# Five of the first loads issued by ScalarE's queue instead of the sync engine's, in a four-layer graph kernel on one core

## What is computed

```python
h = jnp.maximum(_layernorm(x, axis=-1), 0.0)
x = x + _L0_gnn_ref(h, adj, ...)   # H = (adj != 0); relu(conv(h, W1, b1)); layer norm; conv(., W2, b2); + h
h = jnp.maximum(_layernorm(x, axis=-1), 0.0)
x = x + _L1_gnn_ref(h, adj, ...)   # tanh(dinv * A * dinv @ (h @ W) + b)
h = jnp.maximum(_layernorm(x, axis=-1), 0.0)
x = x + _L2_gnn_ref(h, adj, ...)   # scores s = (h @ w) @ a; exp(leaky(8 tanh((s_i + s_j) / 8))) * adj, normalised; @ h @ w
h = jnp.maximum(_layernorm(x, axis=-1), 0.0)
x = x + _L3_gnn_ref(h, adj, ...)   # three times adj @ (x @ W) + b, relu between
```

## Time and profile before

| | |
|---|---|
| median of 3 runs | 1349.94 us (1349.46 to 1351.4) |
| the profiled execution | 1351.4 us, span from first to last instruction 1349.6 us |
| PE busy | 1326.8 us, 98% |
| DVE busy | 1182.8 us, 88% |
| ACT busy | 1048.1 us, 78% |
| POOL busy | 1056.1 us, 78% |
| mean granted clock of TensorE | 0.997 |
| DMA traffic | 64.48 MB, all but the instructions' own on one queue (q1) |

### The profile page before, as it was taken

The page is one execution under the profiler, slowest core; times in us unless marked ns, Lnnn a source line. Parts: engine busy times, 40 slices in busy tenths (PEclk is TensorE's granted clock), DMA queues, the critical chain, the costliest instruction groups (busy, mean ns, idle before and its releaser), DMA issues.

```text
span 1349.6 us, 32286 instructions
## 1 busy us (share of the span) xinstructions
PE 1326.8 (98%) x10680; PEld 1282.2 (95%) x10680; DVE 1182.8 (88%) x3607; ACT 1048.1 (78%) x2632; POOL 1056.1 (78%) x2004
## 2 busy tenths in 40 slices
PE   8899999999999999999999999999999999999988
PEld 7889999999999999999999999999999999999987
DVE  8878898898998898898898898998998998989875
ACT  6776877887887887887887877877877877878864
POOL 7876778778788788788788788788788888888761
PEclk9989999999999999999999999999999999999999
DMA  7011111111111111111111111111111111111100
GB/s 215 21 32 33 44 57 37 48 56 37 48 56 37 48 56 37 48 56 37 48 56 37 48 56 36 49 53 39 49 50 39 52 48 37 56 48 33 33 9 32
DMA packets 83220, 64.48 MB, mean 48 GB/s; under 512 B 40304, under 2 KB 65520, under 8 KB 83056
## 3 DMA queue, kind: packets, MB, share of 16 engines
q1 hardware_dynamic: 83056, 62.43, 15.8%
HBM read 45.62 MB, written 16.78 MB: 46 GB/s over the span
## 4 chain that ended last, share of the span: by engine, by line
PE 89%; DVE 6%; ACT 2%; issue 1%; POOL 1%; DVEq 0%; POOLq 0%; ACTq 0%
PE BANK L351 29%; PE BANK L319 24%; PE BANK L358 14%; PE WIDE L330 8%; PE WIDE L351 8%; PE WIDE L358 4%; PE BANK L304 2%; PE BANK L369 1%; DVE BN_D L535 0%; DVE BN_B L535 0%; DVE BN_A L535 0%; DVE BN_C L535 0%; DVE ULO_B L576 0%; DVE ULO_A L576 0%; ACT H_B L404 0%
## 5 line engine op out<-in xcount | busy, mean ns | idle before, releaser
L576 DVE TENSOR_TENSOR ULO_D<-BANK,UHI_D 128x512 fp32r<-128x512 f32 x96 | 65.6, 684 | 18.6 <-ACT UHI_D L435 18.5
L576 DVE TENSOR_TENSOR ULO_B<-BANK,UHI_B 128x512 fp32r<-128x512 f32 x96 | 65.6, 683 | 17.5 <-ACT UHI_B L435 17.4
L576 DVE TENSOR_TENSOR ULO_A<-BANK,UHI_A 128x512 fp32r<-128x512 f32 x96 | 65.6, 683 | 17.0 <-ACT UHI_A L435 17.0
L576 DVE TENSOR_TENSOR ULO_C<-BANK,UHI_C 128x512 fp32r<-128x512 f32 x96 | 65.5, 683 | 14.1 <-ACT UHI_C L435 14.1
L435 ACT ACTIVATE UHI_C<-BANK 128x512 fp32r<-128x512 f32 x96 | 57.4, 598 | 21.3 <-PE BANK L319 20.1
L435 ACT ACTIVATE UHI_B<-BANK 128x512 fp32r<-128x512 f32 x96 | 57.3, 597 | 20.5 <-PE BANK L319 19.1
L435 ACT ACTIVATE UHI_A<-BANK 128x512 fp32r<-128x512 f32 x96 | 57.4, 598 | 19.5 <-PE BANK L319 18.1
L435 ACT ACTIVATE UHI_D<-BANK 128x512 fp32r<-128x512 f32 x96 | 57.3, 597 | 18.7 <-PE BANK L319 17.4
L705 POOL TENSOR_TENSOR LN_D<-LN_D,MHALF 128x2 f32<-128x2 f32 x80 | 55.7, 696 | 1.3
L705 POOL TENSOR_TENSOR LN_A<-LN_A,MHALF 128x2 f32<-128x2 f32 x80 | 55.7, 696 | 1.3
L705 POOL TENSOR_TENSOR LN_C<-LN_C,MHALF 128x2 f32<-128x2 f32 x80 | 55.6, 695 | 1.3
(11 more groups left out here) (487 smaller groups left out, 5761.5 us busy)
## 6 DMA issues: line engine op xcount, KB each, us to landing
X_A<-in_xs SPq DMA_DIRECT2D x16, 256.0 KB, 2.5
X_B<-in_xs SPq DMA_DIRECT2D x16, 256.0 KB, 2.7
X_C<-in_xs SPq DMA_DIRECT2D x16, 256.0 KB, 2.6
X_D<-in_xs SPq DMA_DIRECT2D x16, 256.0 KB, 2.6
out_rows<-O_A SPq DMA_DIRECT2D x16, 256.0 KB, 2.0
out_rows<-O_B SPq DMA_DIRECT2D x16, 256.0 KB, 2.0
out_rows<-O_C SPq DMA_DIRECT2D x16, 256.0 KB, 2.1
out_rows<-O_D SPq DMA_DIRECT2D x16, 256.0 KB, 2.0
```

Source lines behind the costliest of these rows:

```text
L576: nc.vector.tensor_tensor(ULO[s][:, 0:J * D], bank(s, step, k)[:, :], UHI[s][:, 0:J * D].bitcast(F32), ALU.subtract).then_inc(sem(f"l{step ...
```

## The change

The five loads leave SP's program. ACT issues them, in the same order among themselves, ahead of the first step of its own list. Nothing else is changed: every load has the same source, destination and semaphore, and who waits for it waits for the same count.

```diff
             load("A")
-            sp.dma_start(W1[:, :, :], w1t).then_inc(sem("w1_loaded"), 16)
-            sp.dma_start(COLS[:, :], cols).then_inc(sem("cols_loaded"), 16)
             load("B")
-            sp.dma_start(W2[:, :, :], w2t).then_inc(sem("w2_loaded"), 16)
-            sp.dma_start(L2WT[:, :, :], l2wt).then_inc(sem("l2wt_loaded"), 16)
-            sp.dma_start(B1[:, :], b1.partition_broadcast(P)).then_inc(sem("b1_loaded"), 16)
             load("C")
             sp.dma_start(B2[:, :], b2.partition_broadcast(P)).then_inc(sem("b2_loaded"), 16)
             load("D")
...
+            nc.scalar.dma_start(W1[:, :, :], w1t).then_inc(sem("w1_loaded"), 16)
+            nc.scalar.dma_start(COLS[:, :], cols).then_inc(sem("cols_loaded"), 16)
+            nc.scalar.dma_start(W2[:, :, :], w2t).then_inc(sem("w2_loaded"), 16)
+            nc.scalar.dma_start(L2WT[:, :, :], l2wt).then_inc(sem("l2wt_loaded"), 16)
+            nc.scalar.dma_start(B1[:, :], b1.partition_broadcast(P)).then_inc(sem("b1_loaded"), 16)
             run("ACT", parts)
```

## The result

The changed kernel takes 1353.09 us in the median of 20 runs (1351.81 to 1356.54), the kernel before 1350.26 us (1349.46 to 1354.94). The ratio is 1.0017, with a 95% interval of 1.0009 to 1.0025: slower by some 2.3 us (1.2 to 3.4). That is just inside the 0.2% that I had set as the bound of no change. The median of 1353.09 itself lies 0.1 us above my range; reckoned with the ratio from the 1349.94 that I forecast from, it is 1352.2, inside it. In the later measurements one run of before (1473.29 us) and one of `e7_cols_only` (2694.45 us) were far slower than all the others, and no ratio counts them.

What follows compares the result with a forecast made beforehand. PE, busy 1326.8 of 1349.6 us, was taken to bound the kernel, with the change touching only the start. Terms 0 + 0 + 0 + 0.4 us, added to the median of 1349.94, gave 1350.3 us; range 1347.5 to 1353.0.

Steps and rivals of the forecast that it cites:

- The class: Whole kernel: faster (below 1347.2 us) 0.11, within 0.75, slower (above 1352.6 us) 0.14.
- part 4: Start: two queues share the DMA engines and TF_A lands later; cost 0.4 us.
- rival (b): Start: W1 goes whole ahead of TF_A, delaying it 1.5 us; +1.0 us, 1350.9 us; chance 0.20.
- Part 1: SP's queue: five issues leave, so stream B's loads go about 1.0 us earlier, later streams' about 2.5; worth 0.
- Part 2: Start: the five loads arrive earlier, COLS by up to 1.7 us, with DVE still waiting for UHI_A; gain 0.
- Part 3: ACT's start: five issues, 2.3 us, fit into its 4.17 us of idle time before BHT_A; cost 0.
- d = 0.95 us: Start: assumed delay of TF_A's landing, the middle of 0.4 and 1.5 us.
- equal turns: DMA queues at the start: alternating service puts 128 KB more before TF_A's end, 0.4 us; cost 0.
- slack of 0.55 us: ACT's idle time before G_A, subtracted from TF_A's delay: 0.95 - 0.55 = 0.4 us.
- rival (c): Start: all five loads served before A's, TF_A 4.6 us late, a clock fall behind it; +4.0, 1354.0 us; chance 0.14.
- rival (d): PE between 60 and 100 us: two clock falls don't recur, 3.6 us come back; 1346.3 us; chance 0.11.
- three marks for being wrong: ULO_A before 11 us, a DVE load wait behind 12 us, or PE's 60 to 100 us gaps differing over 2 us.

Runs made afterwards that it cites:

- e7_cols_only: The kernel before with only the COLS load moved to ACT's queue; ratio to before 1.0004 (0.9994 to 1.0014).
- e8: The changed kernel run again without an edit, for a third profile; ratio to before 1.0020 (1.0011 to 1.0029).
- e3: The changed kernel with the five loads issued by ACT only once TF_A has landed, behind the table load; ratio to before 1.0005 (0.9996 to 1.0014).
- e2: The changed kernel run again without an edit, for a second profile; ratio to before 1.0022 (1.0012 to 1.0031).
- e11: The changed kernel run again without an edit, for a fourth profile; ratio to before 1.0015 (1.0006 to 1.0023).
- e6: The changed kernel with only W1 and COLS on ACT's queue, the other three loads back on SP; ratio to before 1.0019 (1.0009 to 1.0029).
- e5: The changed kernel with 22 warm-up matmuls instead of 18; ratio to before 1.0013 (1.0004 to 1.0022).
- e12: The changed kernel with 22 warm-up matmuls instead of 18, measured a second time; ratio to before 1.0009 (1.0000 to 1.0018).
- e1: The kernel before run again without an edit, for a second profile; ratio to before 0.9999 (0.9990 to 1.0008).
- e10: The kernel before run again without an edit, for a third profile; ratio to before 0.9998 (0.9989 to 1.0007).
- e4_start_1us_late: The kernel before with 21 warm-up matmuls instead of 18, no load moved; ratio to before 1.0007 (0.9997 to 1.0016).

## Why the prediction was right, and where not

The class was right, and the mechanism named in part 4 was the one that acted: the change touches only the start, PE fills the middle, and TF_A's delay is carried on. But it was right narrowly. The forecast was 0.4 us over before, and 2.0 to 3.0 us were measured in the four comparisons, beside a bound of 2.7. Both the forecast of +0.4 and the +1.0 of rival (b) were too small.

**Part 1** held in its dates. SP issues TF_B at 2.98 us and TF_C at 5.64. But "stream B's loads are issued 1.0 us earlier" was worth less than nothing: TF_B lands 2.5 us later, behind what ACT's queue had asked for. Its new wait of 2.1 us uses up the slack in front of ULO_A. In the first profile of after DVE reaches ULO_A without any wait, and in e8 it reaches it at 12.40, some 0.1 us after UHI_A is there (11.72 + 0.60).

**Part 2** held, and e7 shows it by itself: the wait for COLS is worth nothing.

**Part 3** held: five issues from 0.73 to 3.09 us, the table load behind them, and ACT still waits 3.4 us for POOL before BHT_A. e3 shows that the issuing costs too little for the ratio to tell.

**Part 4** named the mechanism and mis-sized both of its terms. I took d = 0.95 us, the middle between equal turns and W1 as a whole ahead; measured are 1.45 us in the first profile, and the wait ends at 4.5 us in each of the seven profiles in which W1 was issued at 0.7. That is close to rival (b)'s 1.5, but not by its mechanism. The traces hold every packet with its queue, size and start, and in these loads a packet is one partition's row, 1 KB of TF_A or 4 KB of W1:

| | TF_A's 128 rows start | W1's first row starts | W1's rows started before TF_A's last |
|---|---|---|---|
| before | 1.78 to 2.48 us | 4.09 us | 0 |
| after | 1.76 to 3.76 us | 1.90 us | 108 of 128 |
| e2, e8, e11, e6, e5, e12 | 1.8 to between 3.77 and 3.87 us | 1.88 to 2.17 us | 110 to 116 |

Between 2.9 and 3.4 us of the changed kernel 43 rows of each start. So the queues took equal turns, in rows and not in bytes. The step that failed is "equal turns put 128 KB more before TF_A's end": a turn of W1 is four times as long as one of TF_A, and it was 108 rows, 442 KB, or 1.3 us at the 346 GB/s of the earlier trace rows. That the sum for W1 as a whole comes out near it is luck of the row lengths.

The Trainium skill, DMA: Bandwidth & Descriptors, section Queues, rings and completion order, says that a DMA engine takes turns between queues and empties a whole packet of one, typically 9 to 17 descriptors, before it turns to the next. The trace agrees with the turns. It shows nothing of such long ones: with W1's rows spread evenly over the 16 engines, eight rows of 0.16 us in one go would stop TF_A for 1.3 us, and no two of its starts lie more than 0.17 us apart (the records don't tell the engines apart).

The second term was the slack of 0.55 us. It came from one execution with a long warm-up (over at 7.88 us) and is not there in e1 and e10 (7.3). With d = 1.45 and no slack the working gives 1.45 us; ULO_A moved by 1.5 to 1.9. Of the 0.1 to 0.5 us that are left, a part is the first row, which the prediction leaves out altogether: in before it lands after 2.6 us, long ahead of G, and now after 6.9, and in e2, where it took 7.3, G starts with it at 8.96.

**The clock.** The prediction put the clock at nothing in its sum, and had falls on both sides, as a price behind rival (c) and as the gain of rival (d). This is the term that was missing. Of (c), only the price came, without its delay: falls at 11 to 13 us in two of four profiles of the changed kernel and in none of three of before, and falls at 70 to 73 us in all four against one of three at 68. By the runs sorted by clock, the more frequent falls cost some 0.9 us and the start 1.5 to 1.9. What makes a fall is open. The change isn't needed for one: `e4_start_1us_late` has both without a load moved. The gap of 2.53 us that the earlier trace rows show isn't enough for one: it stands in all 14 profiles at 65 to 69 us, and in five no fall follows. Rival (d)'s 3.6 us do exist: e1 and e10 are the kernel before without its two falls, 3.2 and 3.6 us faster, 0.5 of it from the shorter warm-up. But that is chance between executions, not something that an edit gave.

Of what was to show the forecast, the shift at 44 us came (1.0) and the same shift at 100 us didn't (-0.4), through the falls. One of my three marks for being wrong was met, too: "if ULO_A starts before 11 us" was meant for the changed kernel, but the kernel before itself does it in two of three profiles. I had taken a single profile's date for a property of the kernel.

## What to carry to other kernels

Before moving loads to a second queue, ask which small load the whole start hangs on, and whether a large one will now be served beside it. The second queue gave no bandwidth here (SP's alone had filled the engines to 0.97), and it took away the order in which the loads had been listed: 512 KB issued in the same moment made a load of 128 KB land 1.45 us later. Reckon with turns by row, so with the length of the other load's rows. If the second queue is wanted, hold its large loads back until the small one has landed. Holding all five back, the small COLS too, brought the time back to within 0.05% of before (interval up to 0.14%). And a slack read from one profile is one execution's slack: take a second profile before you subtract it. Where a clock is on record for every run, compare runs of the same clock: that parts what a change costs by itself from what it does to the clock.

## What the runs showed of the hardware

- Two queues with work at the same time were served in turns of about one partition's row, though one had rows of 4 KB and the other of 1 KB: 43 of each started in the same 0.5 us (all 16 DMA engines together).
- The matmuls of most steps 1W (24, moving 256 columns each) run at either 113 or 118 ns apiece, with the clock granted in full. One to four steps of each profile change their pace midway. In thirteen of the fourteen profiles 1 to 5 of some 54 steps 1W between 110 and 1200 us ran at 118; in one 29 did, 2.0 us of that execution. What decides it is open.
- TensorE's granted clock falls to 0.50, 1.2 GHz of 2.4, for 3.4 us at a time, and in two profiles (e11, e12) for 6.8. A fall of 3.4 us costs 1.4 us at 12 us (e2) and 1.5 to 1.7 at 70; the one of 6.8 us in e11 costs 2.4. Most of what spreads the times of before (1347.4 to 1352.7 us) goes with the mean granted clock: medians of 1347.87 us at 1.000, 1349.74 at 0.999 and 1350.72 at 0.997.
- The same 18 warm-up matmuls took 5.9 to 6.8 us from one execution to the next. Their parts are 213 ns apart up to 4.6 us (e11) or as late as 6.4 us (before), and 112 ns from there on.
- A load of 256 pieces of 4 bytes takes 2.5 to 2.6 us to land beside TF_A and X_A of its own queue, and 6.4 to 7.3 us beside 1.6 MB of another queue (4.3 us beside W1 and COLS alone, e6).
